# A causal attention block and a mixture-of-experts block: load order of the weights, and how many turned groups stand ahead of the narrow scores

## What is computed

```python
def _L0_attn_ref(hidden_states, Wq, Wk, Wv, Wo):      # H = 16 heads, HKV = 4, D = 64
    q = (hidden_states @ Wq).reshape(b, s, H, D).transpose(0, 2, 1, 3)
    k = (hidden_states @ Wk).reshape(b, s, HKV, D).transpose(0, 2, 1, 3)
    v = (hidden_states @ Wv).reshape(b, s, HKV, D).transpose(0, 2, 1, 3)
    q = _apply_rope(q, cos, sin)                      # pairs (even, odd) are rotated
    k = _apply_rope(k, cos, sin)
    scores = jnp.einsum('bkgqd,bkpd->bkgqp', qg, k) * scale
    scores = jnp.where(causal, scores, jnp.float32(-1e+30))
    probs = jax.nn.softmax(scores, axis=-1)
    out = jnp.einsum('bkgqp,bkpd->bkgqd', probs, v).reshape(b, H, s, D)
    return out.transpose(0, 2, 1, 3).reshape(b, s, H * D) @ Wo
...
x = x + _layernorm(_L0_attn_ref(_layernorm(x), Wq, Wk, Wv, Wo))
x = x + _layernorm(_L0_ffn_ref(_layernorm(x), ...))   # linear, swiglu, 8 experts (4 used) + shared, linear, swiglu
```

## Time and profile before

| what | value |
|---|---|
| three runs | 1418.61, 1419.69, 1420.23 us; median 1419.69 |
| the profiled execution | 1420.3 us, its span 1418.5 us |
| PE busy | 1317.2 us, 93% of the span |
| DVE, ACT, POOL busy | 978.4 (69%), 776.9 (55%), 376.2 us (27%) |
| PE's score matmuls waiting for ACT's exponentials | 40.8 us in 71 waits |
| SP waiting for raw tiles (L316) | 612.4 us in 91 waits |

### The profile page before, as it was taken

One profiled execution on the slowest core, in us unless ns is written; L12 is line 12 of the kernel. 1 busy time (PEld: TensorE's weight loads), 2 busy tenths in 40 slices (PEclk: granted clock), 3 DMA queues, 4 the chain that ended last, 5 costly groups with the idle time before them and its releaser, 6 DMA issues.

```text
span 1418.5 us, 31011 instructions
## 1 busy us (share of the span) xinstructions
PE 1317.2 (93%) x10432; PEld 926.5 (65%) x10432; DVE 978.4 (69%) x2046; ACT 776.9 (55%) x1708; POOL 376.2 (27%) x412
## 2 busy tenths in 40 slices
PE   3799999999999999999999989999998999999996
PEld 2577777787777776877777777777776644444442
DVE  6577777756777778477777865777776366666665
ACT  3466666646666666366666645666664233333333
POOL 1243444313433433143344322343420000000000
PEclk7899999999999999999999999999999999999999
DMA  4612112011211111112112011212110000000000
GB/s 157 168 41 69 67 48 78 27 57 43 79 37 63 67 42 61 34 40 70 67 48 78 23 60 35 68 48 71 37 53 1 1 1 8 8 7 8 8 8 15
DMA packets 78916, 67.38 MB, mean 47 GB/s; under 512 B 39920, under 2 KB 62192, under 8 KB 78704
## 3 DMA queue, kind: packets, MB, share of 16 engines
q1 hardware_dynamic: 77632, 65.89, 14.3%
q10 hardware_dynamic: 1200, 0.39, 0.1%
HBM read 7.81 MB, written 2.10 MB: 7 GB/s over the span
## 4 chain that ended last, share of the span: by engine, by line
PE 68%; DVE 12%; issue 8%; ACT 7%; SPq 2%; DMA 1%; POOL 1%; DVEq 0%; ACTq 0%; POOLq 0%
PE rows L444 15%; PE o_out L493 13%; PE turn L463 9%; PE rows L634 7%; DVE neg_max L1074 5%; ACT probs L739 4%; PE o_out L657 3%; PE rows L447 3%; PE proj_bank L463 3%; PE o_out L403 2%; PE proj_bank L403 2%; PE proj_bank L386 1%; PE proj_bank L387 1%; PE proj_bank L388 1%; PE turn L469 1%
## 5 line engine op out<-in xcount | busy, mean ns | idle before, releaser
L739 ACT ACTIVATE probs<-rows,neg_max 128x768 f32<-128x768 f32 (+7 forms) x512 | 375.4, 738 | 249.5 <-DVE neg_max L1074 244.3
L1074 DVE TENSOR_REDUCE neg_max<-rows 128x1 f32<-128x768 f32 (+7 forms) x512 | 363.2, 751 | 118.2 <-PE rows L447 118.2
L493 PE MATMUL o_out<-probsT,v_g 128*64 128x128 f32 (+1 forms) x3328 | 280.1, 319 | 0.7 <-DVE probsT L1088 0.7
L493 PEld LDWEIGHTS o_out<-probsT,v_g 128*64 128x64 f32 x3328 | 202.9, 137 | 68.6 <-issue 19.9
L463 PE MATMUL turn<-cf,probs 128*128 128x128 f32 x1792 | 240.2, 274 | 1.3 <-DVE probsT L1088 1.1
L444 PE MATMUL rows<-kk,qh 64*128 64x512 f32 (+2 forms) x768 | 164.9, 426 | 54.4 <-ACT probs L739 40.8
L748 ACT ACTIVATE probsT<-turn 128x512 f32<-128x512 f32 x256 | 153.0, 598 | 110.3 <-PE turn L463 106.5
L463 PEld LDWEIGHTS turn<-cf,probs 128*128 128x128 f32 x1792 | 192.8, 142 | 1.9 <-DVE probsT L1088 1.3
L1088 DVE COPY probsT<-turn 128x512 f32<-128x512 f32 x256 | 174.4, 681 | 1.4 <-PE turn L463 1.1
L940 POOL COPY inv_wide<-inv_sum 128x256 f32<-128x256 f32 x128 | 52.4, 409 | 425.1 <-DVE inv_sum L1080 400.2
L444 PEld LDWEIGHTS rows<-kk,qh 64*128 64x128 f32 x768 | 72.3, 185 | 131.9 <-ACT probs L739 93.3
(11 more groups left out here) (161 smaller groups left out, 1686.1 us busy)
## 6 DMA issues: line engine op xcount, KB each, us to landing
turned<-raw SPq DMA_DIRECT2D x188, 128.0 KB, 2.0
kk<-kk SPq DMA_DIRECT2D x16, 512.0 KB, 2.9
kl<-kl SPq DMA_DIRECT2D x16, 512.0 KB, 3.7
v_g<-v_all SPq DMA_DIRECT2D x32, 256.0 KB, 2.9
slab_a<-w_qk SPq DMA_DIRECT2D x15, 256.0 KB, 2.5
xm<-in_x SPq DMA_DIRECT2D x4, 512.0 KB, 5.0
slab_b<-w_qk SPq DMA_DIRECT2D x16, 128.0 KB, 2.2
out<-xm SPq DMA_DIRECT2D x8, 256.0 KB, 2.3
```

The costliest lines, as they stand in the source:

```text
L493: ins = mm(dst, v_g[p][:, t, :], x, start=t == 0, stop=t == big_w - 1)
L739: A(probs[:, s % 2, q * 128:q * 128 + width], rows[h][:, 0:width], ACT.Exp, bias=neg_max[:, s % 2, item:item + 1], accum_out=exp_sum[:, s ...
L1074: V.tensor_reduce(neg_max[:, s % 2, item:item + 1], rows[h][:, 0:width], AX_X, ALU.max, negate=True).then_inc(max_ready, 1)
```

## The change

It does three things.

1. On SP the tokens of batches 1 to 3 and the first eight weight loads (`EARLY_LOADS`) go out ahead of the wait for the split weights and of `slab_b`. The other twelve are issued two at a time at the end of steps 2 to 7 of batch 0's last group.
2. PE waits for the twenty loads only ahead of batch 1's first output projection (step 1 of its first group).
3. The number of turned groups ahead of the outputs and the narrow scores depends on the step: four in steps 0 and 4, two in steps 7 and 2 (three in the last group's step 2), three in the others. DVE's copies of groups 2 and 3 stand accordingly.

```diff
--- before.py
+++ after.py
@@ -36,6 +36,7 @@
 
 C_ID, C_ONES, C_TIE, C_EPS, C_COS, C_SIN, C_F32 = 0, 128, 192, 256, 257, 257 + S, 257 + 2 * S
 FFN_LOADS = 20
+EARLY_LOADS = 8
 
 CT = HALF // 128
 CHUNKS = B * S // HALF
@@ -69,6 +70,11 @@
     firsts = [*range(mixed, BLOCKS - 2, 4), *range(0, mixed, 4), BLOCKS - 2]
     assert len(firsts) == MOVES
     return [(q, min(q + 4, BLOCKS)) for q in firsts]
+
+
+def groups_first(s, last):
+
+    return 4 if s % STEPS_P == 0 else 2 if s == STEPS_G - 1 or s == 2 and not last else 3
 
 
 def item_of(n, q):
@@ -350,6 +356,9 @@
                     load_values(b, g + 1, 0)
                 for ahead, k in rope_plan(b, s, 0, last):
                     swap_pairs(b, g + ahead, k)
+                if last and b == 0:
+                    for dst, src in loads[EARLY_LOADS + 2 * s - 4:EARLY_LOADS + 2 * s - 2]:
+                        sp.dma_start(dst, src).then_inc(ffn_w_in, 16)
 
             def batch(b):
 
@@ -361,12 +370,12 @@
                 sp.wait_ge(raw_kept, k + 1)
                 for odd in range(2):
                     sp.dma_start(first_turned[k][odd:128:2, :], raw[1 - odd:128:2, k, :]).then_inc(swapped_first[k], 16)
+            for b in range(1, B):
+                sp.dma_start(xm[:, b * TILES:b * TILES + TILES, :], x_v[b]).then_inc(x_in[b], 16)
+            for dst, src in loads[:EARLY_LOADS]:
+                sp.dma_start(dst, src).then_inc(ffn_w_in, 16)
             sp.wait_ge(w_split, 1)
             move(slab_b[:], w_qk[:, :, 0, 256:384]).then_inc(slab_b_in, 16)
-            for b in range(1, B):
-                sp.dma_start(xm[:, b * TILES:b * TILES + TILES, :], x_v[b]).then_inc(x_in[b], 16)
-            for dst, src in loads:
-                sp.dma_start(dst, src).then_inc(ffn_w_in, 16)
             for b in range(B):
                 batch(b)
             for n in range(CHUNKS):
@@ -500,7 +509,7 @@
                 g1, s1 = earlier(g, s, 1)
                 g2, s2 = earlier(g, s, 2)
                 if depth > 0:
-                    for j in range(3):
+                    for j in range(groups_first(s, last)):
                         turn_probs(b, g1, s1, j, last and s > 2)
                 if depth > 1:
                     outputs(b, g2, s2, 0, TILES)
@@ -510,8 +519,8 @@
                     turn_tokens(b + 1, 0, proj_bank)
                 score_rows(b, g, s, 0)
                 if depth > 0:
-                    for j in range(3, MOVES):
-                        turn_probs(b, g1, s1, j)
+                    for j in range(groups_first(s, last), MOVES):
+                        turn_probs(b, g1, s1, j, last and s > 2)
                     turn_kept(pe, step_index(b, g1, s1), 2)
                 if turns:
                     pe.wait_ge(x_split if b + 1 < B else x2_kept, 2 * b + 3 if b + 1 < B else 1)
@@ -519,6 +528,8 @@
                 first = isinstance(g, int) and g == 0 and b > 0
                 if first and s == 1:
                     pe.wait_ge(o_kept, step_index(b, 0, 0) + 1)
+                    if b == 1:
+                        pe.wait_ge(ffn_w_in, 16 * FFN_LOADS)
                     project_out(0, proj_bank)
                     project_out(1, o_out)
                     pe.wait_ge(wo_kept, 2 * b - 1)
@@ -565,8 +576,6 @@
                 project_first(k, rows[k % 2][:, k // 2 * HALF:k // 2 * HALF + HALF])
             pe.wait_ge(cb_ready, 1)
             for b in range(B):
-                if b == 1:
-                    pe.wait_ge(ffn_w_in, 16 * FFN_LOADS)
                 steps(pe, b, lambda *at: step(b, *at))
             drain(B - 1)
             outputs(B - 1, HKV - 1, STEPS_G - 1, 0, TILES)
@@ -1111,14 +1120,20 @@
                 row_maxima(b, g, s, 1)
                 if depth > 0:
                     keep_turned(b, g1, s1, 1)
-                    keep_turned(b, g1, s1, 2)
+                    if groups_first(s, last) > 2:
+                        keep_turned(b, g1, s1, 2)
                 if depth > 1:
                     keep_outputs(b, *earlier(g, s, 2))
+                if depth > 0 and groups_first(s, last) > 3:
+                    keep_turned(b, g1, s1, 3)
                 if last and s == 2 and b + 1 < B:
                     split_tokens(b + 1, 0, proj_bank)
                 row_maxima(b, g, s, 0)
                 if depth > 0:
-                    keep_turned(b, g1, s1, 3)
+                    if groups_first(s, last) < 3:
+                        keep_turned(b, g1, s1, 2)
+                    if groups_first(s, last) < 4:
+                        keep_turned(b, g1, s1, 3)
                 if last and s == 2 and b + 1 < B:
                     split_tokens(b + 1, 1, proj_bank)
                 if isinstance(g, int) and g == 0 and s < 2:
```

## The result

The changed kernel takes 1410.53 us (median of 6 runs, 1405.26 to 1413.80), the kernel before 1419.49 us on the same chip (6 runs, 1418.61 to 1422.06): a ratio of 0.9931, 95% interval 0.9909 to 0.9953. The forecast was 1409.4, with a range of 1402 to 1416.5.

The account below looks back on a forecast made before the run. PE, busy 93% of the span, was taken as the bound, leaving only its waits and low clock. Profiled 1420.3 − 7.1 (head) − 3.2 (groups) = 1410.0 us, 1409.4 against the median; range 1402 to 1416.5.

Parts of the forecast that it names:

- The head: First group: projection 4's swap issued earlier removes PE's 5.83 us wait and half-clock time; 7.1 us gained, bounds 4 to 8.
- The clock in the head: First group, step 2: a new 1.2 us PE wait leaves the clock full, as a 1.99 us wait had.
- The loads in `slab_b`'s way: Start of the kernel: early loads ahead of `slab_b` could delay it by 0 to 1.3 us; taken as 0.
- The twelve late loads: Batch 0's last group, steps 2 to 7: two loads issued behind each step's swap cost nothing.
- The groups: All groups of the loop: moving turned groups between steps gains 0.2 us per group, 3.2 us in all.
- The walk through a group: Undisturbed group: steps 7 and 0 together gain 0.3 us, step 2 loses 0.04, step 4 loses 0.05.
- The waits: Undisturbed group: PE waits 0.6 to 0.7 us ending step 7, 0.4 step 2, about 0.25 before step 5's narrow scores.
- 1: Loop groups: half the copies' delays are passed on, 0.3 us lost per group, 4.8 in all; 1417.4 us; chance 13%.
- 2: Steps 0 and 4: group 3's copy delays VectorE's chain by 0.61 us, 0.73 lost per group; 1424.3 us; chance 4%.
- Rival 3: Steps 7 and 2: group 2's copy never holds PE, 0.67 and 0.41 us better per group; 1392; 10% including in-between.
- 4: First group: clock falls or `slab_b` lands late, 3 or 1.3 us less gained; 1412.4 or 1410.7 us; chance 10%.
- 5: First group: something other than the swap held `proj_bank`, so only the turned groups' gain remains; 1416.5 us; chance 3%.

Follow-up runs that it names:

- step 4 as before: The changed kernel with three turned groups ahead in step 4 and four only in step 0: 1411.07 us, ratio 0.9922 to the kernel before.
- Groups alone: The changed kernel with all loads issued as before, keeping only the split of turned groups by step: 1417.41 us, ratio 0.9979 to the kernel before.

## Why the prediction was right

- **The head** (7.1 us): right in mechanism and place, and in this execution in size. The swap went out at 38.41 (said: 37.5; its raw tile was kept later, since `wk` landed 0.9 us later in this execution, in code that the change leaves alone), the new wait ended at 55.29 (said: 55.4), the clock stayed full, and step 3's second piece came at 58.50 (said: 58.7). 7.3 us. Two steps of it were not as the prediction has them. The wait was 1.65 and not 1.2, over the 1.5 that was to show it wrong: I had put group 2 in front of step 2's outputs (0.5 us), though the change itself moves it behind. It costs nothing, as the exponentials end the wait in both cases. And I looked for what held PE behind the raw copy, but not at `v_g`, which came only some 2 us ahead of it; that the same loads held both was luck.
- **The clock in the head** was luck in part. I had taken from one profile that a wait of 1.99 us leaves it full. In this execution the same wait, ahead of 46.77, did so again. But in six of the fourteen profiles the half level followed within 1.6 us of that wait, as in the kernel with step 4 as before, whose code is the same up to there (the wait, then the window with the clock of 0.53):

```profile
48.08 0.58 PE L453 MATMUL rows<-kk,qh 64*128 64x256 f32 x2 [1.99 <-ACT probs L748]
```

```profile
48.00:50.00 2.00, 1.92 (x12) 1.70 (x13) 0.69 (x3) 0.62 (x4) 0.00 (x0) 0.53 0.00 0
```

In three such profiles, where the clock had also risen later before that, step 3's second piece came at 60.22 to 60.83, so the head's gain would have read 5.0 to 5.6 us there: within the bounds of 4 to 8, and not the 7.3.
- **The loads in `slab_b`'s way** (0): right, with a few tenths of delay hidden. Its projection came at 36.05, later than the 35.3 that was to show the loads in its way, but that is again the 0.9 us of `wk`: it followed the narrow scores' last matmul (35.90) without a wait.
- **The twelve late loads** (0): right. Batch 0's end shows no wait of PE for a swap.
- **The groups** (3.2 us): the sum was near, its terms were not, and that they met is luck. Groups alone gave 3.5 us by the medians, on top of the loads 2.7, and 1.3 by block 2. An undisturbed group gave 0.46 us, where I had 0.2. But sixteen such groups would make 7.4 us, and much of it is given back: with the groups alone, from step 5 to step 5, a batch's first group gained less than 0.1 us on average, and each passage to the next batch lost 0.5. I had counted them like the others and did not walk them, though DVE has more to do there.
- **The walk through a group** failed in one kind of step. For a wait inside a piece of scores I took the number in the bracket: 0.44 and 0.43. The time lost is from start to start: 1.40 us in the row at 164.98, where the same two pieces now stand 0.80 apart (157.07, 157.87). The wait was 0.60, as the first piece's drain of 0.16 lay under it. The same again in step 3 (0.46 apart now). Against that, PE woke 0.24 us behind the end of DVE's copy (156.83 to 157.07) and 0.15 in step 3, where I had 0.06. These make 0.32 gained and 0.26 lost; another 0.2 of the 0.27 that I missed lies in small steps of 0.07 to 0.13.
- **The waits** themselves came as said: 0.79 and 0.43 for the copy of group 2 (said: 0.6 to 0.7 and 0.4), none ahead of step 0's narrow scores, 0.18 ahead of step 5's (0.25), and step 4's move worth nothing.
- **Rivals.** 1 and 2 (the groups cost) fall to the loops of 60.5. Of 2, DVE's order is a real cost, but of 0.25 a group, where that rival had it turn the group into a loss of 0.73. Rival 3 did not come, and its size was too large: the wait for copy 2 taken away gave 0.65 a group, where I had 1.08. 4: neither the clock nor the slab in this execution; the clock fell in the head of others, above. 5: what the loads held was the cause.
- **The clock in the second block** was in no term. Attention gained 10.9 us in the profile (I had 10.3), the medians 8.96. In the profile the execution's gain is only 6.5, and what is missing is the second block's 4.4 us of low clock. Whether that explains the medians as well, I can't say: only profiled executions show it. But the shortest of the six runs (1405.26) has the highest mean clock (0.994) and the longest the lowest (0.987).

## What to carry to other kernels

Look for what is issued in front of the first transfer that something waits for, in a queue written by hand: each load holds it for its issue (0.4 to 2.5 us here), and a wait can cost the clock as well: the 5.8 us here brought some 3 more at the half level. Look also at what else stands in that queue (`v_g` here). When work is moved past another's wait, look at the two places where it is given back: the copy's new place on the other engine, and the wait that frees its buffer. Both could be moved here, and were worth two times the move itself. Read a gain per group at the ends too, where other work joins.

## What the runs showed of the hardware

- The same code got its clock differently. PE's wait of 2.08 us at the start of the second block was followed by the half level (1.2 GHz) in the profiles of five kernels out of fourteen, by the full one (2.4 GHz) in nine. And the fall towards the end came 15 to 16 us ahead of the end of the span in six (after among them, row 1396:1398) and 4 to 7 us ahead of it in the other eight. With neither, the second block took 301.3 to 301.4 us (seven profiles), with one of them or both 303.1 to 306.0. I found nothing in PE's work ahead of these places that tells the two apart. It is up to 4.6 us, more than most of the differences studied here; what decides it stays open.
- The same holds in the head: a wait of 1.99 us, at the same place of all fourteen profiles, was followed by the half level in six.
- A median landing says little of a single transfer: issued behind eight loads, `slab_b` landed after 2.4 to 3.1 us, with no weight load ahead after 2.3 or 2.4; the second transfer of one swap landed after 2.2 us in after, and after 3.7 and 4.0 in two kernels with no load near it.
- The issue of `w_o` (512 KB) took SP 2.51 us after and 1.59 before, the three of the tokens (512 KB each) 1.90 together, that of `slab_b` (128 KB) 0.70: the time does not follow the bytes. Behind all twenty loads, `slab_b` was issued 7.6 us later than in after and landed 2.3 us after its issue: their issue held it, not their bytes.
